# One TensorE and ScalarE reordering in a graph layer: each round's node units ahead of its edge work

## The reference

```
msg = concat(x[src], edge_attr) @ W1 + b1          # per edge, 128 wide
agg = segment_sum(msg, dst)                        # per node
out = concat(x, agg) @ W2 + b2                     # per node, 64 wide
result = layernorm(x + out)                        # over the 64 features
```

## Time and profile before

| | |
|---|---|
| median of the runs | 711.47 us |
| the profiled execution | 712.24 us |
| its span in the trace | 710.3 us |
| TensorE busy (matmul) | 566.6 us, 80% |
| VectorE busy | 519.7 us, 73% |
| ScalarE busy | 397.4 us, 56% |
| GpSimd busy | 398.9 us, 56% |
| TensorE's granted clock, mean | 0.907 of full speed |

### The profile page before, as it was taken

One profiled execution on the slowest core, in us unless ns is written; L12 is line 12 of the kernel. 1 busy time (PEld: TensorE's weight loads), 2 busy tenths in 40 slices (PEclk: granted clock), 3 DMA queues, 4 the chain that ended last, 5 costly groups with the idle time before them and its releaser, 6 DMA issues. The chain is left out here.

```text
span 710.3 us, 28935 instructions
## 1 busy us (share of the span) xinstructions
PE 566.6 (80%) x8370; PEld 507.2 (71%) x8371; DVE 519.7 (73%) x1820; ACT 397.4 (56%) x2012; POOL 398.9 (56%) x418
## 2 busy tenths in 40 slices
PE   1365798998888888898889888898888888873774
PEld 1355687888777877787778878787777777763653
DVE  2684677778788877778778778778888888863443
ACT  0011478777777777777777777776544445532101
POOL 5777657777757777766774777765744444000000
PEclk9955799999999999999999999999999999985555
DMA  2122345545545555545555545554433333220002
GB/s 63 33 38 38 81 123 147 136 120 132 147 117 149 127 124 138 141 122 126 142 136 136 133 120 131 139 132 114 99 83 81 81 81 96 81 59 7 2 1 60
DMA packets 168746, 71.33 MB, mean 100 GB/s; under 512 B 61570, under 2 KB 162447, under 8 KB 168720
## 3 DMA queue, kind: packets, MB, share of 16 engines
q1 hardware_dynamic: 104592, 51.74, 25.5%
q0 software_dynamic: 12544, 12.87, 9.8%
q10 hardware_dynamic: 51584, 6.41, 5.8%
HBM read 45.37 MB, written 25.60 MB: 100 GB/s over the span
## 5 line engine op out<-in xcount | busy, mean ns | idle before, releaser
L381 POOL DMA_INDIRECT feat<-in_x,src_idx x392 | 391.9, 1000 | 197.9 <-issue 117.7
L806 DVE TENSOR_SCALAR onehot<-node_of_col,group_base,dst_of 128x256 bf16<-128x256 bf16 x944 | 288.0, 349 | 90.8 <-issue 81.2
L490 PEld LDWEIGHTS ps_y<-z_window,onehot 128*128 128x128 bf16 x5664 | 195.1, 100 | 48.8 <-DVE z_window L809 30.2
L490 PE MATMUL ps_y<-z_window,onehot 128*128 128x64 bf16 x5664 | 213.5, 196 | 18.0 <-DVE z_window L809 14.1
L596 ACT ACTIVATE square<-ps_y 128x64 bf16<-128x64 f32 x784 | 162.1, 238 | 94.7 <-PE ps_y L481 91.9
L596 ACT ACTIVATION_READ_ACCUMULATOR square<-ps_y 128x1 f32 x784 | 159.1, 224 | 0.0
L417 PE MATMUL ps_z<-wz,feat_t 97*128 97x64 f32 x784 | 106.0, 293 | 31.5 <-DVE z_rest L725 31.4
L481 PE MATMUL ps_y<-wx,x_t 128*128 128x128 f32 x784 | 114.9, 291 | 18.5 <-ACT x_t L589 12.7
L417 PEld LDWEIGHTS ps_z<-wz,feat_t 97*128 97x128 f32 x784 | 100.3, 207 | 40.3 <-DVE z_rest L725 36.5
L809 DVE COPY z_window<-z 128x384 bf16 x472 | 121.6, 258 | 0.0
L481 PEld LDWEIGHTS ps_y<-wx,x_t 128*128 128x128 f32 x784 | 99.1, 197 | 22.3 <-ACT x_t L589 16.5
(11 more groups left out here) (113 smaller groups left out, 214.3 us busy)
## 6 DMA issues: line engine op xcount, KB each, us to landing
xin<-in_x SPq DMA_DIRECT2D x97, 256.0 KB
out<-yout SPq DMA_DIRECT2D x97, 256.0 KB
feat<-in_x,src_idx POOLq DMA_INDIRECT x392
feat<-in_edge_attr ACTq DMA_DIRECT2D x96, 64.0 KB
z<-in_src SPq DMA_DIRECT2D x1, 192.0 KB
z<-in_dst SPq DMA_DIRECT2D x1, 192.0 KB
xin<-in_x SPq DMA_DIRECT2D x1, 128.0 KB
out<-yout SPq DMA_DIRECT2D x1, 128.0 KB
```

Source lines behind the costliest of these rows:

```text
L381: nc.gpsimd.indirect_dma_start(out=feat[h][:, feat_at(k) + feat_slot(c), 0:C], out_offset=None, in_=x[:, :], in_offset=bass.IndirectOffset ...
L490: mm = nc.tensor.matmul(ps_y[h][:, col:col + C], onehot[h][:, g, s, a, :], z_window[h][:, g, s, part * C:(part + 1) * C], start=False, sto ...
L806: ins = nc.vector.tensor_scalar(onehot[h][:, g, s, :, :], node_of_col[:, :, :], base, dst_of[:, bass.ds(firsts[g] + (at + s), 1)], ALU.add ...
```

## The change

In every round the order of the two halves is exchanged on TensorE and on ScalarE: the units of row k-2 are run first, and the edge round k (with `z_mids(k-2)` on ScalarE) second. The last rounds, written out behind the loops, follow the same order. VectorE, GpSimd and SyncE are unchanged, and so are all instructions and all waits: none is added and none is taken away.

```
--- before.py
+++ after.py
@@ TensorE
             with pe.Fori(LAG + 2, PAIRS - 1) as k:
+                for_units(pe, mybir.EngineType.PE, k - LAG, unit)
                 edge_round(k)
-                for_units(pe, mybir.EngineType.PE, k - LAG, unit)
+            for_units(pe, mybir.EngineType.PE, PAIRS - 1 - LAG, unit)
             edge_round(PAIRS - 1)
-            for_units(pe, mybir.EngineType.PE, PAIRS - 1 - LAG, unit)
             for h in range(2):
                 message(PAIRS - 1, h)
@@ ScalarE
             with act.Fori(LAG + 2, PAIRS - 2) as k:
+                for_units(act, mybir.EngineType.Activation, k - LAG, unit)
                 edge_round(k)
                 z_mids(k - 2)
-                for_units(act, mybir.EngineType.Activation, k - LAG, unit)
+            for_units(act, mybir.EngineType.Activation, PAIRS - 2 - LAG, unit)
             keep_feat(PAIRS - 2, 0)
             load_ea(PAIRS - 1, 0)
             keep_feat(PAIRS - 2, 1)
             load_ea_last()
             z_highs(PAIRS - 3)
             z_mids(PAIRS - 4)
-            for_units(act, mybir.EngineType.Activation, PAIRS - 2 - LAG, unit)
+            for_units(act, mybir.EngineType.Activation, PAIRS - 1 - LAG, unit)
             for h in range(2):
                 keep_feat(PAIRS - 1, h)
             z_highs(PAIRS - 2)
             z_mids(PAIRS - 3)
-            for_units(act, mybir.EngineType.Activation, PAIRS - 1 - LAG, unit)
             z_highs(PAIRS - 1)
             z_mids(PAIRS - 2)
             for_units(act, mybir.EngineType.Activation, PAIRS - LAG, unit)
```

## The result

The changed kernel takes 929.13 us (928.76 to 929.65, four runs) against 711.81 us of the kernel before on the same chip (710.66 to 714.82): a ratio of 1.3045, 95% interval 1.3004 to 1.3086. It is slower by 217 us; forecast were 956 us, 915 to 1010. The profiled execution has a span of 926.9 us, 216.6 more than before.

The account below looks back on a forecast made before the run. VectorE was taken to set the round, so its stall is paid in full: 197 + 41 + 7 = 245 us on the profiled 712.24 gives 957, with 0.8 off for the median 956 us; range 915 to 1010.

Parts of the forecast that it names:

- VectorE bounds, and holding it up is paid in full: In the long middle VectorE sets the round of 10.83 us; TensorE and ScalarE follow, so its stalls cost fully.
- The wait falls on z_lows, through ScalarE's chain: VectorE's z_lows waits for ScalarE's z_mids some 43 times, 5 us each, over 200 us together.
- The chain's terms: From W, a unit's last z window copy end, through ScalarE's work to z_lows at W+7.15, before W+1.85: 5.3 us stall.
- The gap won back: VectorE's table reading partly runs on during the wait before z_lows: 0.2 us won back, leaving 5.1 a round.
- Rival A: VectorE's sequencer works ahead in the wait, hiding its issue gaps: 3.7 to 4 us a round, 903 us; 7%.
- The clock: the step that was mis-sized: TensorE idles over 4 us, starts each unit at half clock: 0.7 us more in single-pair rounds, a round of 5.8.
- the distance of two z_lows: Sign on VectorE: from one z_lows to the next in the middle should be 16 to 17 us.
- The rule of the Trainium skill: A TensorE waiting longer between bursts starts each burst throttled; without the rule the sum would be 24 us lower.
- Rounds and tail: Round 5 nothing, rounds 6 to 39 197 us, 40 to 47 41 us, round 48 6.7 us; last unit unchanged.
- What costs nothing: GpSimd's gathers, ScalarE's edge loads, SyncE's loads and stores stay covered; a two-unit round pays the stall once.
- Rival C: TensorE's stall on z_rest was the round's cost; its removal gains up to 31.4 us, 680 us; 2%.

Follow-up runs that it names:

- table_early: Masked kernel before, with VectorE reading the second block's table in three pieces between first-block one-hots, the first block's behind z_lows and z_rests: 998.59 us.
- mid_twice: One more ScalarE copy ahead of z_mids, against the masked kernel of each order: old order 715.71 against 715.18 us, new order 971.95 against 937.62.
- z_first: Masked changed kernel with z_highs(k-1) and z_mids(k-2) ahead of the two keep_feat on ScalarE: 882.51 us.
- both_first: Masked changed kernel with ScalarE's z_mids(k-2) ahead of the units and z_highs(k-1) ahead of the two keep_feat: 820.33 us.
- filled: Masked changed kernel with 18 unused bf16 matmuls between turn_x and each unit's first block sum on TensorE: 944.29 us.
- act_alone: Masked changed kernel with TensorE's loop put back to the order of before, so only ScalarE is moved: 1057.7 us.
- mid_twice_after: Masked changed kernel with one more ScalarE copy of the same size just ahead of z_mids: 971.95 us against 937.62.
- dve_along: Masked changed kernel with VectorE's units also ahead of its z rows and all units one table row later (k-3): 741.82 us.

## Why the prediction was right, and by how much it was off

- *VectorE bounds, and holding it up is paid in full.* Right: z_lows starts at W+6.94 in place of W+1.85, 5.09 us later; 0.29 are won back behind it, and a round without clock loss is 4.75 us longer. table_early shows the same from another cause. With the clock's part the mean over the rounds 6 to 38 is 5.07 us.
- *The wait falls on z_lows, through ScalarE's chain.* Right: 277.0 us in 48 waits, 4 of them there before (43 forecast, over 200 us). The two mid_twice kernels, z_first and both_first show that ScalarE's copies stand on it, the added one by its 0.52 us and a further cost through the clock.
- *The chain's terms.* Measured against forecast, from W: dense ends 1.55 (1.56), squares 1.58 (1.60), first keep_feat 3.85 (4.01), second 4.64 (4.95), z_highs 5.55 (5.96), z_mids ends 6.66 (7.07), z_lows 6.94 (7.15). The first keep_feat can start under the root, and behind it the spacings are 0.79 and 0.91 in place of 0.94 and 1.01. I had taken the first spacing from a row in which keep_feat itself waited for TensorE (the 0.34 in the earlier trace rows); such a row bounds a spacing from above only. The second had an issue gap of 0.41 before z_highs, which is 0.31 here.
- *The gap won back.* 437.18 - 434.86 = 2.32 against 2.61: 0.29, not 0.2. So a round without any clock loss is 15.62 us, 4.75 over the old mean of 10.87; forecast 5.1. Rival A is out: of the gap of 0.97 there remain 0.69.
- *The clock: the step that was mis-sized.* I took 0.7 us for every single-unit round. The forecast chain was nearly exact for the rounds that it hits: in the round before the z_lows at 419.24, with W at 411.47, the unit ends at W+2.33 (2.4 forecast) and the round is 16.44 us. But only one round in three is like that; the other two are 15.6 and 15.7, just under the 16 to 17 us that I had named as the distance of two z_lows. Such a round on TensorE (the burst behind the idle stretch, and the dense that ends the unit), then the windows of the clock, with the columns of the earlier trace rows:

```profile
406.06 2.86 PE L490 MATMUL ps_y<-z_window,onehot 128*128 128x64 bf16 x48 [4.65 <-DVE z_window L809]
...
412.66 1.14 PE L481 MATMUL ps_y<-wx,x_t 128*128 128x128 f32 x8
```

```profile
408.00:410.00 2.00, 2.00 (x23) 1.98 (x21) 1.38 (x7) 0.00 (x0) 0.44 (x1) 0.50 0.09 18
410.00:412.00 2.00, 2.00 (x31) 1.66 (x31) 1.97 (x9) 1.18 (x12) 0.00 (x0) 0.61 0.00 0
...
424.00:425.00 1.00, 1.00 (x23) 0.98 (x20) 0.41 (x2) 0.00 (x0) 0.81 (x1) 0.50 0.16 33
425.00:426.00 1.00, 1.00 (x13) 1.00 (x11) 0.90 (x4) 0.00 (x0) 0.00 (x0) 0.90 0.15 33
```

The clock came back late in 410 to 412, over 5 us after the burst began, as the earlier trace rows had led me to expect (there the unbroken work began at 657.63, so the return took some 6 us and not 5.7); in the round that follows TensorE's burst at 422.43 it came back early in 425 to 426, after some 3 us. The length of the idle stretch doesn't sort the two: it is 4.65 us before the late one and 4.93 before the early one. What decides it, no run here shows. The mean over the rounds 6 to 38 is about 0.3 us, and filled gives 0.29 by another way. This term is 34 x 0.4 = 14 us of the 28 by which the forecast was too high; the shorter chain makes the most of the rest, 42 x 0.35 = 15. Both terms were too high, so no luck of signs brought the total within 3%.

The rule of the Trainium skill ("TensorE: Matmul & The Clock Gate", "HAM oscillation — how this bites in real kernels") holds by the trace of the changed kernel: each burst behind the idle stretch starts at the half clock (0.50), but most of the loss lies under VectorE's pace. both_first, with its short idle stretch of 2.02 us, is another case: its burst starts at the full clock and the fall comes inside it.

- *Rounds and tail.* Right: round 5 costs 1.9 us (0), rounds 39 to 46 4.5 each, the tail from round 47 on 11.5 (11.8), the last unit nothing.
- *What costs nothing.* Right for this change (one wait of 1.9 us on the edge loads), but act_alone shows that the cover of the edge loads depends on both engines being moved.
- *Rival C* is out: TensorE's wait for z_rest did vanish, 27 us of it, and gave nothing, since it had been slack of an engine that follows VectorE.

## What to carry to other kernels

Ahead of exchanging two halves of a round, write down for each in-order engine what stands in front of the work that the others need, and how many steps of cover lie between its producer and that place; moving a producer behind one step of other work can take all of it, though no wait is added and no instruction changes. The busy share named TensorE, but the engine without real waits was VectorE, and its stall was the price. Read spacings of a chain from rows in which the instruction did not wait. And before taking a kernel as a test, write out the sequence that each engine then runs: dve_along looked like a third order and was the first one again.

## What the runs showed of the hardware

One register operation more at each read of the units' table costs about 2 us of 713 in the old order and 8.5 us of 929 in the new. A read of six table values on VectorE, cut in three, costs more than in one piece (gaps of 0.30 to 0.35 us each against 0.73 once, a round of 11.43 against 10.95 us).

The price of TensorE's idling through the clock doesn't follow the length of the idling. With 4.4 to 4.9 us of it the unit ends late, by about 0.8 us, in one round of three; with about 5.5 us (mid_twice_after) in every round, by about 0.8; and with 2.0 us (both_first) in every round too, by 0.6. A fall of the clock can also come inside a burst: in both_first it came over 2 us after TensorE had begun again.

An issue gap of 6.4 us ahead of an instruction appeared in every round when VectorE's loop held its unit twice; its cause is open.
